# A graph attention kernel on one core: the slot table from one side of the comparison, and smaller first pieces of x and W_ah

## Chip, core and metric

One core of a Trainium2 chip. The metric is the device time of one execution in microseconds (us); runs of the same kernel are compared by their median.

## The reference

A graph network over N = 1250 nodes with D = 768 features and 41,250 edges (`src`, `dst`), the edges sorted by `dst`; the network adds a loop to every node.

```python
x1 = relu(x @ W_ah + b_ah)
for W, a_src, a_dst, b in three layers:           # 4 heads of 192 features
    h = (x1 @ W).reshape(N, 4, 192)
    e = leaky_relu((h * a_src).sum(-1)[src] + (h * a_dst).sum(-1)[dst], 0.2)
    alpha = softmax of e over the edges of each dst
    xs.append(relu(segment_sum(alpha * h[src], dst) + b))
y = relu(concatenate(xs) @ W_out + b_out)
out = layernorm(x + y)
```

## The kernel before

The attention is done densely: for each destination the kernel counts how often each source occurs (`cntT`, 1250 x 1250) and works with matrices after that. The start of the kernel makes these counts and, interleaved with them, x1.

*Counts.* The destinations are cut into NW = 105 windows of 12. Since the edges are sorted, the edges of a window are a run of the edge list. The **slot table** says where each window's run begins; 512 edges from there are loaded for each window (`load_slots`, L343, in 7 batches, the first of 4 windows). VectorE (DVE) turns them into key columns (`key_columns`, L853 to L861) and one-hot matrices (L865), two windows (one `unit`) at a time, three buffers deep. TensorE (PE) multiplies the one-hots into counts (L1131, L1148), ScalarE (ACT) moves the counts out (L580, L586).

*The slot table.* `dst` is loaded 330 edges to a partition, ten groups of 33. DVE takes the highest and the lowest destination of each group (L806, L807), compares them with every window's ends for two sides, the start of a run (side 0, `reaches[:, 0]`) and its end (side 1, `reaches[:, 1]`) (L808 to L811), and folds the ten groups to one (`reach`, L813 to L816). PE transposes both sides (L1181), DVE reduces over the partitions into `ab[:, 0:2]` (L820) and adds both for the run's length in `ab[:, 2]` (L822); PE lays both out as rows (L1184, L1185), and DVE makes the table from the first (L824). The second row, the lengths, is used only for the number of passes of a loop that takes edges beyond the 512 (L886 to L893).

*x1.* 108 steps (`x1_step`, L1172; six steps of 128 features to one output block, at two matmul instructions each). PE's order is written out by hand: two steps, the transposes of `reach`, the rows, steps up to the twelfth (`X1_HEAD`), and then a unit of counts, some steps, a unit, and so on, 53 units in all. ACT moves each finished block out (L604, L605) and asks for the W_ah piece after next.

*Queues.* ACT's DMA queue carries W_ah block 0 (L558, 384 KB), x for the first four tiles in three parts of 500 KB (L570; `G0_PARTS`) and W_ah block 1. SP's queue carries `dst` (L348) and two small biases, and, once the second x part is there, the vector a of layer 0 (L356, 768 KB) and the first 128 rows of W_all (L364, 384 KB). It then waits for the table and issues the edge loads.

*DVE's order* after the table: eight products of W_all with a (`reduce_v(0, 0)`, L839), then for each batch the key columns and one-hots; the loop counts come after batch 0. The other 136 products follow the last one-hot; PE's scores (L1209) wait for the last of them and for x1. The layers and the output follow.

Every step of DVE's table chain waits for the one before (`link`).

Of the kernel before, what the change touches and what calls it, by code (L numbers as in the profile page):

```python
# [14 lines left out]
PT = 125  # L15
NT = N // PT
KP = 128
KT = D // KP
LH = LAYERS * HEADS
WD = 12  # L20
NW = -(-N // WD)
# [22 lines left out]
G0_PARTS = 3  # L44
# [57 lines left out]
def gnn_program(nc, x, xT_rows, dst, edges, W_ah, b_ah, W_all, a_all, b_all, W_out, b_out, out):  # L102
# [10 lines left out]
    with ExitStack() as ctx:  # L113
# [3 lines left out]
        def sem(name):  # L117
            return ctx.enter_context(nc.semaphore(name))
# [180 lines left out]
        x0_in = [sem(f"x0_in{i}") for i in range(G0_PARTS)]  # L299
        x_in = [sem(f"x_in{g}") for g in range(len(GROUPS))]  # L300
        wah_in = [sem(f"wah_in{m}") for m in range(KT)]
# [45 lines left out]
        def _(sp):  # L347
            sp.dma_start(e_int, dst.rearrange("o (p e) -> p (o e)", p=PT)).then_inc(S["edges_in"], 16)  # L348
            sp.dma_start(b_ah_sb[:], b_ah).then_inc(S["small_in"], 16)
# [16 lines left out]
            sp.wait_ge(x0_in[G0_PARTS - 2], 16)  # L366
# [188 lines left out]
        def _(act):  # L555
# [10 lines left out]
            load_w_ah(0)  # L566
            for i in range(G0_PARTS):
                kk = slice(KT // G0_PARTS * i, KT // G0_PARTS * (i + 1))
                wide = GROUPS[0][1] * PT
                act.dma_start(xT[0][:, kk].rearrange("p k n -> p (k n)"),  # L570
                              xT_rows[:, kk.start * wide:kk.stop * wide]).then_inc(x0_in[i], 16)
# [216 lines left out]
        def _(dve):  # L788
            n = [0]

            def link(ins):
# [14 lines left out]
            link(nc.vector.tensor_reduce(highest, groups, axis=AX.X, op=ALU.max))  # L806
            link(nc.vector.tensor_reduce(lowest, groups, axis=AX.X, op=ALU.min))  # L807
            nc.vector.tensor_tensor(reaches[:, 0], over_w(highest), win_lo_g, ALU.is_ge)  # L808
            link(nc.vector.tensor_tensor(reaches[:, 1], win_hi_g, over_w(lowest), ALU.is_ge))
            nc.vector.tensor_tensor(reaches[:, 0], reaches[:, 0], over_w(to_end), ALU.mult)  # L810
            link(nc.vector.tensor_tensor(reaches[:, 1], reaches[:, 1], over_w(group_end), ALU.mult))  # L811
            rows = lambda v: v.rearrange("p s w g -> p (s w) g")
            link(nc.vector.tensor_tensor(rows(reach4), rows(reaches)[:, :, 0:4], rows(reaches)[:, :, 4:8], ALU.max))  # L813
            link(nc.vector.tensor_tensor(rows(reach2), rows(reach4)[:, :, 0:2], rows(reach4)[:, :, 2:4], ALU.max))
            link(nc.vector.tensor_tensor(rows(reach_g), rows(reach2), rows(reaches)[:, :, 8:GP], ALU.max))
            nc.vector.tensor_tensor(reach.rearrange("p s w -> p (s w)"), rows(reach_g)[:, :, 0], rows(reach_g)[:, :, 1],  # L816
                                    ALU.max).then_inc(S["reach_sb"], 1)

            dve.wait_ge(S["reachT_ps"], 1)
            link(nc.vector.tensor_reduce(ab[:, 0:2], bank(2)[0:NW, 0:256].rearrange("p (w c) -> p w c", w=2)[:, :, 0:PT],  # L820
                                         axis=AX.X, op=ALU.max))
            nc.vector.tensor_tensor(ab[:, 2:3], ab[:, 0:1], ab[:, 1:2], ALU.add).then_inc(S["ab_sb"], 1)  # L822
            dve.wait_ge(S["rows_ps"], 1)
            nc.vector.tensor_scalar(table[0:1, 0:NW], bank(3)[0:1, 0:NW], -float(GE), float(EDGES), ALU.mult, ALU.add  # L824
                                    ).then_inc(S["table_sb"], 1)

# [43 lines left out]
            for k in range(V_HEAD):  # L870
                reduce_v(0, k)
            dve.sem_inc(S["more_read"], 1)
            dve.wait_ge(S["consts_made"], 3)
            for i, (w0, mid, w1) in enumerate(BATCHES):
# [10 lines left out]
                if i == 0:  # L885
                    link(nc.vector.tensor_reduce(longest[0:1, 0:1], bank(3)[0:1, NW:2 * NW], axis=AX.X, op=ALU.max))  # L886
# [235 lines left out]
        def _(pe):  # L1122
# [36 lines left out]
            def x1_step(s):  # L1159

                i, k = s // KT, s % KT
                m, g = X1_ORDER[i]
                o, w = GROUPS[g][0] * PT, GROUPS[g][1] * PT
                if k == 0:
                    if i >= 3:
                        pe.wait_ge(S["turn_sb"], i - 2)
                    pe.wait_ge(wah_in[m], 16)
                    if g > 0:
                        pe.wait_ge(x_in[g], 16)
                if i == 0 and k % (KT // G0_PARTS) == 0:  # L1170
                    pe.wait_ge(x0_in[k // (KT // G0_PARTS)], 16)
# [262 lines left out]
```

## Time and profile before

| what | value |
|---|---|
| median of 3 runs | 964.36 us (963.82 to 965.69) |
| profiled execution, whole | 963.98 us |
| profiled execution, span from first to last instruction | 962.4 us |
| PE busy (matmuls) | 937.6 us, 97% of the span |
| DVE busy | 739.8 us, 77% |
| ACT busy | 366.8 us, 38% |

The span is what the trace covers; the rest of an execution's time lies around it. Shares of busy time are averages over stages with different limits, and a busy PE is one that has work in it, at whatever pace. In the rows below PE stands for matmuls and PEld for the weight loads that run beside them; SPq and ACTq are DMA issues on the queues of those engines.

### The profile page before, as it was taken

What the parts mean: (1) busy time and instruction counts of PE and PEld (TensorE: products, weight loads), DVE (VectorE), ACT (ScalarE), POOL (GpSimd) and SP (SyncE); (2) the same over time, 40 slices, a digit from 0 to 9 for tenths busy, and PEclk for the clock granted to TensorE, in tenths of its full rate; (3) what the DMA queues carried; (4) which work ended last, traced back from release to release, by engine and by line L of the source; (5) the groups of instructions that cost most, each with busy time, mean ns of one, the idle gap of its engine ahead of it and who ended that gap; (6) DMA issues with size and microseconds to landing.
All of it is one profiled execution on the core that took longest, in us unless ns stands there. A gap on an engine that the chain in (4) does not pass through costs nothing. (4 is left out here: it accounts for less than half of the span.)

```text
span 962.4 us, 14549 instructions
## 1 busy us (share of the span) xinstructions
PE 937.6 (97%) x5662; PEld 869.3 (90%) x5662; DVE 739.8 (77%) x1064; ACT 366.8 (38%) x534; POOL 45.8 (5%) x94
## 2 busy tenths in 40 slices
PE   6999999999999999999999999999999999999997
PEld 2677649999999999999999999999999879999996
DVE  6999986999999299989989988988877282243233
ACT  1566322122212245465555555555555450011000
POOL 4600000000000000010010010010010100000000
PEclk9999999999999999999999999999999999999999
DMA  6350722534442822153252362239331263223211
GB/s 181 55 183 19 259 85 91 165 115 143 140 153 89 229 82 82 64 126 79 84 120 62 93 130 58 78 87 375 101 103 60 87 169 129 81 85 113 75 33 32
DMA packets 57692, 108.16 MB, mean 112 GB/s; under 512 B 14012, under 2 KB 41245, under 8 KB 56486
## 3 DMA queue, kind: packets, MB, share of 16 engines
q1 hardware_dynamic: 39188, 66.22, 22.7%
q0 software_dynamic: 5360, 18.77, 8.0%
q10 hardware_dynamic: 13090, 22.44, 7.5%
q8 instruction: 34, 0.56, 0.2%
q14 instruction: 20, 0.16, 0.1%
HBM read 80.34 MB, written 27.08 MB: 112 GB/s over the span
## 5 line engine op out<-in xcount | busy, mean ns | idle before, releaser
L1311 PE MATMUL ps<-R_W 125*125 125x193 f32 x2400 | 397.8, 327 | 5.0 <-ACT R_XIN L722 3.9
L1311 PEld LDWEIGHTS ps<-R_W 125*125 125x125 f32 x2400 | 391.3, 188 | 8.7 <-ACT R_XIN L722 7.6
L707 ACT ACTIVATE R_W<-R_EXP,s 125x1250 f32<-125x1250 f32 x120 | 161.2, 1344 | 162.3 <-PE ps L1311 93.9
L998 DVE SCALAR_TENSOR_TENSOR R_W<-R_W,R_CNT 125x1250 f32<-125x1250 f32 x120 | 174.4, 1453 | 3.9 <-DVE R_EXP L987 2.0
L957 DVE CUSTOM_DVE_ANT_0 R_ROWS<-R_MASK,R_ROWS 125x1250 bf16<-125x1250 bf16 x100 | 138.6, 1453 | 3.2 <-ACTq L660 3.2
L1228 PE MATMUL ps<-Wl_hi,x_hi 128*125 128x384 f32 x360 | 122.1, 339 | 0.0
L1228 PE MATMUL ps<-Wl_hi,x_lo 128*125 128x384 f32 x360 | 121.7, 338 | 0.0
L1228 PE MATMUL ps<-Wl_lo,x_hi 128*125 128x384 f32 x360 | 121.6, 338 | 0.0
L1370 PE MATMUL ps<-Wo_hi,xs_hi 128*125 128x384 f32 (+2 forms) x324 | 109.5, 338 | 0.3 <-PE ps L1360 0.3
L1370 PE MATMUL ps<-Wo_lo,xs_hi 128*125 128x384 f32 (+2 forms) x324 | 109.4, 338 | 0.0
L1370 PE MATMUL ps<-Wo_hi,xs_lo 128*125 128x384 f32 (+2 forms) x324 | 109.2, 337 | 0.0
L987 DVE SCALAR_TENSOR_TENSOR R_EXP<-R_EXP,s 125x1250 f32<-125x1250 f32 x60 | 90.7, 1514 | 21.1 <-DMA R_EXP<-u_dram 12.2
L987 DVE SCALAR_TENSOR_TENSOR R_EXP<-R_X,s 125x1250 f32<-125x1250 f32 x60 | 90.6, 1510 | 18.4 <-ACT R_W L707 18.0
L1102 DVE TENSOR_TENSOR R_EXP<-ps,R_EXP 125x768 f32<-125x768 f32 (+2 forms) x11 | 9.7, 884 | 99.0 <-PE ps L1370 99.0
L680 ACT COPY R_HOUT<-ps 125x384 f32<-125x384 f32 x60 | 28.9, 481 | 140.3 <-PE ps L1228 138.7
L1172 PE MATMUL ps<-R_W 128*128 128x500 f32 (+1 forms) x180 | 73.8, 540 | 7.6 <-DMA R_W<-in_xT 7.6
L1228 PEld LDWEIGHTS ps<-Wl_hi,x_hi 128*125 128x125 f32 x360 | 66.8, 185 | 0.5 <-issue 0.4
L1228 PEld LDWEIGHTS ps<-Wl_lo,x_hi 128*125 128x125 f32 x360 | 66.7, 185 | 0.0
L1228 PEld LDWEIGHTS ps<-Wl_hi,x_lo 128*125 128x125 f32 x360 | 66.7, 185 | 0.0
L785 ACT ACTIVATE rstd<-mv,epsc 125x1 f32<-125x1 f32 x10 | 3.0, 295 | 158.6 <-DVE mv L1113 158.6
L865 DVE TENSOR_TENSOR R_EXP<-R_EXP 128x2000 f16<-128x2000 f16 (+1 forms) x53 | 59.7, 1185 | 2.7 <-PE ps L1148 2.4
L1370 PEld LDWEIGHTS ps<-Wo_hi,xs_hi 128*125 128x125 f32 x324 | 60.0, 185 | 1.8 <-issue 0.9
(146 smaller groups left out, 854.0 us busy)
## 6 DMA issues: line engine op xcount, KB each, us to landing
xs_dram<-R_XIN POOLq DMA_DIRECT2D x18, 625.0 KB, 9.3
h_dram<-R_HOUT ACTq DMA_DIRECT2D x30, 336.0 KB
R_W<-h_dram SPq DMA_DIRECT2D x12, 840.0 KB
R_ROWS<-as_dram SPq DMA_DIRECT2D x12, 625.0 KB, 4.4
R_EXP<-u_dram SPq DMA_DIRECT2D x6, 1250.0 KB, 6.4
R_X<-u_dram SPq DMA_DIRECT2D x6, 1250.0 KB, 5.8
R_ROWS<-in_W_all SPq DMA_DIRECT2D x18, 384.0 KB, 3.5
Wo_sb<-in_W_out POOLq DMA_DIRECT2D x1, 6912.0 KB, 27.3
```

Source lines behind the costliest of these rows:

```text
L680: nc.scalar.copy(h_out[:, slot, t % 2 * HALF:(t % 2 + 1) * HALF], bank((2 * c + t) % 4)[0:PT, 0:HALF]).then_inc(S["h_sb"], 1)
L707: nc.scalar.activation(prob[r % PSLOTS], expo[:, r % XSLOTS], ACT.Exp, bias=s02[:, r % NT, ds(2 * p + r // NT, 1)]).then_inc(S["exp_done"], 1)
L785: nc.scalar.activation(rstd[:, t % 2, 0:1], mv[:, t % 2, 1:2], ACT.Sqrt, bias=epsc[:, 0:1]).then_inc(S["std_done"], 1)
L865: return nc.vector.tensor_tensor(slot.rearrange("p (b q c) -> p b q c", b=blocks, c=EPR), cols.unsqueeze(1).broadcast_to((KP, blocks, PT * ...
L957: nc.vector.tensor_tensor_reduce(out=masked[:, i % 2], in0=mask[:, b], in1=asB[0:PT, hh % 2], scale=1.0, scalar=NOBODY, op0=ALU.add, op1=A ...
L987: nc.vector.scalar_tensor_tensor(out=expo[:, r % XSLOTS], in0=uB[q][0:PT, 0], scalar=s08[:, r % NT, ds(2 * p + q, 1)], in1=uB[q][0:PT, 1], ...
L998: nc.vector.scalar_tensor_tensor(out=prob[r % PSLOTS], in0=prob[r % PSLOTS], scalar=HUGE, in1=cntT[:, r % NT, 0:N], op0=ALU.min, op1=ALU.m ...
L1102: nc.vector.tensor_tensor(yt_part, y_part, bo_part, ALU.add).then_inc(S["y_sum"], 1)
L1172: ins = mm(bank(5 + i % 3)[:, 0:w], W_ah_sb[m][:, k], xT[g][:, k], start=(k == 0), stop=(k == KT - 1))
L1228: ins = mm(place, xx[:, k, t * PT:(t + 1) * PT], ww[n][:, k], start=(k == 0 and i == 0), stop=(k == blocks[-1] and i == 2), skip_group_che ...
L1311: ins = mm(ps[0:PT, o:o + HW], prob[r % PSLOTS][:, t * PT:(t + 1) * PT], hB[:, q, j], start=(j == 0 and t % 2 == 0), stop=(j == NT - 1), s ...
L1370: ins = mm(place, xx[i][:, k], ww[:, k, half], start=(k == 0 and n == 0), stop=(k == OK - 1 and n == 2))
```

## The change

The table is made from side 0 alone, and side 1, with the lengths, is worked out behind it. W_ah block 0 is loaded in two pieces: its first 128 columns of the 768 in front of x on ACT's queue, the rest on SP's queue behind `dst`. The first x group comes in four parts, of 1, 1, 2 and 2 of its six blocks, where there were three parts of 2. PE does four x1 steps ahead of the first transpose where it did two, the second transpose after nine, and the row of lengths after twelve. DVE folds each side by itself, compares side 1 between the first reduction and the table, and reduces and adds the lengths after `reduce_v(0, 0)`.

```diff
-G0_PARTS = 3
+X0_CUTS = (0, 1, 2, 4, 6)
+X0_PARTS = list(zip(X0_CUTS, X0_CUTS[1:]))
+BEFORE_TABLE = 4
+BEFORE_LENGTHS = 9
...
             sp.dma_start(e_int, dst.rearrange("o (p e) -> p (o e)", p=PT)).then_inc(S["edges_in"], 16)
+            sp.dma_start(W_ah_sb[0][:, 1:KT].rearrange("p k f -> p (k f)"), W_ah[0][:, KP:KT * KP]).then_inc(wah_in[0], 16)
...
-            sp.wait_ge(x0_in[G0_PARTS - 2], 16)
+            sp.wait_ge(x0_in[len(X0_PARTS) - 2], 16)
...
-            load_w_ah(0)
-            for i in range(G0_PARTS):
-                kk = slice(KT // G0_PARTS * i, KT // G0_PARTS * (i + 1))
+            act.dma_start(W_ah_sb[0][:, 0], W_ah[0][:, 0:KP]).then_inc(wah_first, 16)
+            for i, (k0, k1) in enumerate(X0_PARTS):
                 wide = GROUPS[0][1] * PT
-                act.dma_start(xT[0][:, kk].rearrange("p k n -> p (k n)"),
-                              xT_rows[:, kk.start * wide:kk.stop * wide]).then_inc(x0_in[i], 16)
+                act.dma_start(xT[0][:, k0:k1].rearrange("p k n -> p (k n)"),
+                              xT_rows[:, k0 * wide:k1 * wide]).then_inc(x0_in[i], 16)
...
+            def fold(side):
+
+                link(nc.vector.tensor_tensor(reach4[:, side], reaches[:, side, :, 0:4], reaches[:, side, :, 4:8], ALU.max))
+                link(nc.vector.tensor_tensor(reach2[:, side], reach4[:, side, :, 0:2], reach4[:, side, :, 2:4], ALU.max))
+                link(nc.vector.tensor_tensor(reach_g[:, side], reach2[:, side], reaches[:, side, :, 8:GP], ALU.max))
+                nc.vector.tensor_tensor(reach[:, side], reach_g[:, side, :, 0], reach_g[:, side, :, 1], ALU.max
+                                        ).then_inc(S["reach_sb"], 1)
+
+            link(nc.vector.tensor_tensor(reaches[:, 0], over_w(highest), win_lo_g, ALU.is_ge))
+            link(nc.vector.tensor_tensor(reaches[:, 0], reaches[:, 0], over_w(to_end), ALU.mult))
+            fold(0)
             link(nc.vector.tensor_reduce(lowest, groups, axis=AX.X, op=ALU.min))
...
+            dve.wait_ge(S["reachT_ps"], 1)
+            nc.vector.tensor_reduce(ab[:, 0:1], bank(2)[0:NW, 0:PT], axis=AX.X, op=ALU.max).then_inc(S["ab_sb"], 1)
             link(nc.vector.tensor_tensor(reaches[:, 1], win_hi_g, over_w(lowest), ALU.is_ge))
...
             dve.wait_ge(S["rows_ps"], 1)
             nc.vector.tensor_scalar(table[0:1, 0:NW], bank(3)[0:1, 0:NW], -float(GE), float(EDGES), ALU.mult, ALU.add
                                     ).then_inc(S["table_sb"], 1)
+            link(nc.vector.tensor_tensor(reaches[:, 1], reaches[:, 1], over_w(group_end), ALU.mult))
+            fold(1)
...
             for k in range(V_HEAD):
                 reduce_v(0, k)
+            dve.wait_ge(S["reachT_ps"], 2)
+            dve.wait_ge(S["ab_sb"], 1)
+            link(nc.vector.tensor_reduce(ab[:, 1:2], bank(2)[0:NW, 128:128 + PT], axis=AX.X, op=ALU.max))
+            nc.vector.tensor_tensor(ab[:, 2:3], ab[:, 0:1], ab[:, 1:2], ALU.add).then_inc(S["ab_sb"], 1)
...
                 if i == 0:
+                    dve.wait_ge(S["rows_ps"], 2)
...
-                    pe.wait_ge(wah_in[m], 16)
+                    pe.wait_ge(wah_first if i == 0 else wah_in[m], 16)
...
+                if i == 0 and k == 1:
+                    pe.wait_ge(wah_in[0], 16)
+                if i == 0 and k in X0_CUTS:
+                    pe.wait_ge(x0_in[X0_CUTS.index(k)], 16)
...
-            for s in range(KT // G0_PARTS):
+            for s in range(BEFORE_TABLE):
                 x1_step(s)
-            pe.wait_ge(S["reach_sb"], 1)
-            for w in range(2):
-                ins = nc.tensor.transpose(bank(2)[0:NW, w * 128:w * 128 + PT], reach[:, w], ident[0:PT, 0:PT])
-            ins.then_inc(S["reachT_ps"], 1)
-            pe.wait_ge(S["ab_sb"], 1)
-            mm(bank(3)[0:1, 0:NW], ab[:, 0:1], ident[0:NW, 0:NW], start=True, stop=True)
-            mm(bank(3)[0:1, NW:2 * NW], ab[:, 2:3], ident[0:NW, 0:NW], start=True, stop=True).then_inc(S["rows_ps"], 1)
-
-            for s in range(KT // G0_PARTS, X1_HEAD):
+            reach_turn(0)
+            table_row(0)
+            for s in range(BEFORE_TABLE, BEFORE_LENGTHS):
                 x1_step(s)
+            reach_turn(1)
+            for s in range(BEFORE_LENGTHS, X1_HEAD):
+                x1_step(s)
+            table_row(2)
```

`reach_turn(side)` waits for `reach` of that side and transposes it; `table_row(column)` waits for that column of `ab` and lays it out as a row.

## Rows read from the trace of the kernel before

**Rows 1.** The chain that ended last, page, share of the span by engine.

```profile
PE 24%; ACT 0%; DVE 0%; issue 0%; ACTq 0%
```

**Rows 2.** Timeline, loads and first steps: start, duration, instruction, idle and releaser.

```profile
0.97 0.38 SPq L348 DMA_DIRECT2D R_CNT<-in_dst  x1
...
1.40 1.43 ACTq L570 DMA_DIRECT2D R_W<-in_xT  x3
...
7.58 3.67 PE L1172 MATMUL ps<-R_W 128*128 128x500 f32 x4 [7.58 <-DMA R_W<-in_xT]
...
8.54 0.34 PEld L1172 LDWEIGHTS ps<-R_W 128*128 128x128 f32 x1 [0.50 <-issue]
8.71 0.33 SPq L356 DMA_DIRECT2D R_ROWS<-in_a_all  x1
...
9.38 0.34 PEld L1172 LDWEIGHTS ps<-R_W 128*128 128x128 f32 x1 [0.50 <-issue]
```

**Rows 3.** Timeline, DVE from dst to reach.

```profile
5.66 0.33 DVE L804 CAST R_CNT<-R_CNT 125x330 f32<-125x330 int32 x1 [1.19 <-DMA R_CNT<-in_dst]
6.02 0.50 DVE L806 TENSOR_REDUCE R_CNT<-R_CNT 125x10 f16<-125x330 f32 x1
...
7.08 0.71 DVE L808 TENSOR_TENSOR R_CNT<-R_CNT 125x1050 f16<-125x1050 f16 x1
...
9.80 0.62 DVE L813 TENSOR_TENSOR R_CNT<-R_CNT 125x840 f16<-125x840 f16 x1
10.46 0.38 DVE L814 TENSOR_TENSOR R_CNT<-R_CNT 125x420 f16<-125x420 f16 x1
10.87 0.54 DVE L815 TENSOR_TENSOR R_CNT<-R_CNT 125x420 f16<-125x420 f16 x1
11.44 0.38 DVE L816 TENSOR_TENSOR R_CNT<-R_CNT 125x210 f32<-125x210 f16 x1
```

**Rows 4.** Timeline, the exchange between PE and DVE for the table.

```profile
11.87 0.46 PE L1181 MATMUL ps<-ident,R_CNT 125*105 125x125 f32 x2 [0.62 <-DVE R_CNT L816]
12.37 0.42 DVE L820 TENSOR_REDUCE ab<-ps 105x2 f32<-105x250 f32 x1 [0.55 <-PE ps L1181]
12.83 0.16 DVE L822 TENSOR_TENSOR ab<-ab 105x1 f32<-105x1 f32 x1
...
13.49 8.65 PE L1172 MATMUL ps<-R_W 128*128 128x500 f32 x20
13.60 0.26 DVE L824 TENSOR_SCALAR table<-ps 1x105 int32<-1x105 f32 x1 [0.61 <-PE ps L1185]
```

**Rows 5.** Timeline, DVE from the table to the loop counts.

```profile
15.26 0.36 DVE L839 CUSTOM_DVE_ANT_0 R_EXP<-R_ROWS 128x192 bf16<-128x192 f32 x1 [1.41 <-DMA R_ROWS<-in_W_all]
...
17.51 0.07 DVE L839 DVE_READ_ACCUMULATOR2_ANT u_place<- 128x1 f32 x1
...
18.04 0.18 DVE L853 CAST R_EXP<-R_EXP 128x32 f32<-128x32 int32 x1 [0.46 <-DMA R_EXP<-in_edges]
...
19.21 2.31 DVE L865 TENSOR_TENSOR R_EXP<-R_EXP 128x2000 f16<-128x2000 f16 x2
...
21.44 0.25 DVE L886 TENSOR_REDUCE longest<-ps 1x1 int32<-1x105 f32 x1
```

**Rows 6.** Timeline, PE at unit 0, units 2 and 6, and the scores.

```profile
21.98 0.39 PE L1131 MATMUL ps<-R_EXP 128*125 128x120 f16 x4
...
25.19 0.45 PE L1131 MATMUL ps<-R_EXP 128*125 128x120 f16 x4 [0.97 <-DVE R_EXP L865]
...
31.02 0.42 PE L1131 MATMUL ps<-R_EXP 128*125 128x120 f16 x4 [0.50 <-DVE R_EXP L865]
...
129.96 12.77 PE L1209 MATMUL ps<-R_X,u_place 128*24 128x500 f32 x36 [0.49 <-issue]
```

**Rows 7.** Waits of DVE, 31.1 to 132 us; one window, busy by engine.

```profile
DVE R_EXP L865 <- PE ps L1148: 2.4, 6, 0.9
...
31.10:150.00 118.90, 118.37 (x847) 79.41 (x848) 108.90 (x356) 58.64 (x110) 11.13 (x38) 1.00 0.41 127
```

More of the change, by code:

```diff
@@ L298, in gnn_program @@
         S = {n: sem(n) for n in names}
-        x0_in = [sem(f"x0_in{i}") for i in range(G0_PARTS)]
+        x0_in = [sem(f"x0_in{i}") for i in range(len(X0_PARTS))]
         x_in = [sem(f"x_in{g}") for g in range(len(GROUPS))]
+        wah_first = sem("wah_first")
         wah_in = [sem(f"wah_in{m}") for m in range(KT)]
@@ L807, in _ @@
+            link(nc.vector.tensor_tensor(reaches[:, 0], over_w(highest), win_lo_g, ALU.is_ge))
+            link(nc.vector.tensor_tensor(reaches[:, 0], reaches[:, 0], over_w(to_end), ALU.mult))
+            fold(0)
             link(nc.vector.tensor_reduce(lowest, groups, axis=AX.X, op=ALU.min))
-            nc.vector.tensor_tensor(reaches[:, 0], over_w(highest), win_lo_g, ALU.is_ge)
+            dve.wait_ge(S["reachT_ps"], 1)
+            nc.vector.tensor_reduce(ab[:, 0:1], bank(2)[0:NW, 0:PT], axis=AX.X, op=ALU.max).then_inc(S["ab_sb"], 1)
@@ L809, in _ @@
             link(nc.vector.tensor_tensor(reaches[:, 1], win_hi_g, over_w(lowest), ALU.is_ge))
[L810 to L821, printed above, removed]
@@ L822, in _ @@
-            nc.vector.tensor_tensor(ab[:, 2:3], ab[:, 0:1], ab[:, 1:2], ALU.add).then_inc(S["ab_sb"], 1)
             dve.wait_ge(S["rows_ps"], 1)
@@ L1166, in x1_step @@
                         pe.wait_ge(S["turn_sb"], i - 2)
-                    pe.wait_ge(wah_in[m], 16)
+                    pe.wait_ge(wah_first if i == 0 else wah_in[m], 16)
                     if g > 0:
                         pe.wait_ge(x_in[g], 16)
-                if i == 0 and k % (KT // G0_PARTS) == 0:
-                    pe.wait_ge(x0_in[k // (KT // G0_PARTS)], 16)
+                if i == 0 and k == 1:
+                    pe.wait_ge(wah_in[0], 16)
+                if i == 0 and k in X0_CUTS:
+                    pe.wait_ge(x0_in[X0_CUTS.index(k)], 16)
                 ins = mm(bank(5 + i % 3)[:, 0:w], W_ah_sb[m][:, k], xT[g][:, k],
@@ L1175, in x1_step, with reach_turn, table_row @@
                     ins.then_inc(S["turn_ps"], 1)
-            for s in range(KT // G0_PARTS):
-                x1_step(s)
-            pe.wait_ge(S["reach_sb"], 1)
-            for w in range(2):
-                ins = nc.tensor.transpose(bank(2)[0:NW, w * 128:w * 128 + PT], reach[:, w], ident[0:PT, 0:PT])
-            ins.then_inc(S["reachT_ps"], 1)
-            pe.wait_ge(S["ab_sb"], 1)
-            mm(bank(3)[0:1, 0:NW], ab[:, 0:1], ident[0:NW, 0:NW], start=True, stop=True)
-            mm(bank(3)[0:1, NW:2 * NW], ab[:, 2:3], ident[0:NW, 0:NW], start=True, stop=True).then_inc(S["rows_ps"], 1)
-            for s in range(KT // G0_PARTS, X1_HEAD):
+            def reach_turn(side):
+                pe.wait_ge(S["reach_sb"], side + 1)
+                nc.tensor.transpose(bank(2)[0:NW, side * 128:side * 128 + PT], reach[:, side], ident[0:PT, 0:PT]
+                                    ).then_inc(S["reachT_ps"], 1)
+            def table_row(column):
+                pe.wait_ge(S["ab_sb"], 1 if column == 0 else 2)
+                o = 0 if column == 0 else NW
+                mm(bank(3)[0:1, o:o + NW], ab[:, column:column + 1], ident[0:NW, 0:NW], start=True, stop=True
+                   ).then_inc(S["rows_ps"], 1)
+            for s in range(BEFORE_TABLE):
+                x1_step(s)
+            reach_turn(0)
+            table_row(0)
+            for s in range(BEFORE_TABLE, BEFORE_LENGTHS):
                 x1_step(s)
+            reach_turn(1)
+            for s in range(BEFORE_LENGTHS, X1_HEAD):
+                x1_step(s)
+            table_row(2)
             for un in range(NU):
```

## The prediction

> **What bounds the kernel now.** I read the chain of waits first. It follows back only the last quarter of the span, all of it in the output product [rows 1], so it says nothing of the start, where the whole edit lies. So I took the timeline from 0 to 45 us, engine by engine, and then asked where the start meets the rest: the waits of PE and DVE behind it, and the busy time of a long window.
>
> The start is three threads. PE cannot begin before the first x piece lands, at 7.58 us; it does two steps, stops for `reach` at 11.87, stops again for `ab`, and runs ten steps from 13.49 [rows 2, 4]. DVE gets `dst` at 5.66, finishes both sides of `reach` at 11.82 (11.44 + 0.38), and writes the table from 13.60 to 13.86 [rows 3, 4]. Behind the table stand the edge loads, and DVE takes up the first edges at 18.04. Meanwhile it does the eight products on W_all, from 15.26, when W_all has landed, to 17.58 [rows 5]. The reader should see that DVE is free only 0.46 us before the edges are there.
>
> From 18.04 DVE runs without a break into the one-hots (19.21), the loop counts (21.44) and the next batch. PE reaches unit 0 at 21.98, although its one-hots were ready near 20.4 (19.21 and half of 2.31). But then it waits 0.97 us for DVE before 25.19, and 0.50 before 31.02 [rows 6]. So up to 31 us DVE sets the pace. From there PE is busy 118.37 of 118.90 us, while DVE waits for PE six times, 2.4 us in all [rows 7]. Both meet again at 129.96, where PE stands 0.49 us [rows 6]: the scores need DVE's last product. What the edit does to the end is therefore how far it moves DVE's first key columns, now at 18.04, and with them one-hots and PE at 31 us. The rest hangs on that like a rigid bar.
>
> **The change part by part.**
>
> *Loads.* Step 0 needed 384 + 500 KB of the ACT queue, beside 173 KB on SP's: 1057 KB in all by 7.58 us. `x0_in[1]`, 500 KB on, lets SP issue at 8.71 [rows 2]: 442 KB per us. `dst` (161 KB, with at least as much of the other queue beside it) was usable at 5.66 [rows 3], which makes 383 KB per us up to 7.58. Step 0 now needs 64 + 250 KB, with as much moved for SP (`dst`, then the 320 KB rest of W_ah): 628 KB, hence 5.66 + 306/383 = 6.5 us. Bounds: 5.7 (as early as `dst`) and 7.6 (no gain). Step 1 needs x part 1 and the W_ah rest, 1057 KB again, so 7.6; step 0 runs until 8.2 and hides that. Steps 2 and 3 need what let SP issue at 8.71 and start later. The bytes ahead of the a and W_all loads are the same and SP's wait names the same x rows, so I keep W_all at 15.26. Bounds: 0.5 us earlier (two queues full from the start) and 0.3 later (smaller pieces).
>
> *PE ahead of the table.* A slow step costs 2 x 0.84 = 1.67 us (weight loads at 8.54 and 9.38 [rows 2]); the steps from 13.49 are twice as fast, 20 instructions in 8.65 us, less their tail 0.42 each, 0.84 a step [rows 4]. These are the paces of the two levels, 1.2 and 2.4 GHz. PE was slow from 7.58 at least until its fourth matmul, which began near 10.2, some 3.67 us of work in all. I let it be slow for 3.8 us again: from 6.5, two steps at 1.67 (9.84), step 2 half and half (1.25, 11.09), step 3 0.84: 11.93. `reach_turn(0)` then comes at 11.93, where the transposes now start at 11.87: the head start is spent on the two added steps.
>
> *DVE ahead of the table.* `reach` of side 0 is ready long before: highest (ends 6.52), comparison and product 2 x 0.71, then the four folds at half size, about 9.4 us with gaps of 0.03 [rows 3]. That 2.4 us gain goes into waiting for PE. Fold prices: 840 elements took 0.62 and 420 took 0.38, so 0.57 ns an element on 0.14 fixed; the halves cost 0.38, 0.26, 0.34 (from 0.54) and 0.26 (from 0.38), 1.24 instead of 0.96 for half the work.
>
> The Trainium skill, "VectorE: DVE Perf Modes", section "The TRN2 errata", speaks against such a split: operations out of SBUF pay a fixed extra time per instruction, so small tiles should be avoided. The rows agree (the 0.14 above); if the time went by elements alone, the sum below would be 0.28 smaller.
>
> *The exchange.* Now from 11.87: reduction at 12.37, sum 0.16, table at 13.60. After: one transpose, reduction at 11.93 + 0.31 = 12.24 for about 0.28 (half of 0.42, plus the fixed part), to 12.52. Then the comparison of side 1, 0.71, sits between reduction and table on DVE: to 13.22. The row comes back from PE 0.43 after the reduction (the 0.61 of now, 12.99 to 13.60, less two matmuls), at 12.95, hidden. Table 13.25 to 13.51: **0.35 us earlier** than 13.86. Edges land as long after it as now (4.18): 17.69.
>
> *DVE behind the table.* Moved here: product 0.70, four folds 1.24, five gaps 0.15: 2.09, ends 15.60. W_all is there at 15.26, so the eight products (2.32) run 15.60 to 17.92. Then the second reduction 0.28, the sum 0.16 and their gaps 0.06: 18.42. The edges have landed. The key columns start near 18.45, **0.4 us later than 18.04**. So the gap DVE stood idle in (13.86 to 15.26, 17.58 to 18.04, 1.86 us) is filled with 2.59 us of moved work, and only 0.35 is won by the early table.
>
> *New waits.* `reach_turn(1)` stands on PE behind nine steps, about 17.2 (12.95 and five steps); side 1 is ready at 15.6, and the transpose is there at 17.5 when DVE asks for it at 17.92, 0.4 to spare. `table_row(2)` waits for `ab` at 18.4, and PE gets there after three more steps and the transpose, near 19.8; its row, at 20.1, is wanted only by DVE's loop counts, at 21.44 + 0.4. Queued behind it stand PE's units, whose first one-hots are ready at 20.8. So all three cost nothing, and from the named slack on they cost what is over. ACT's third W_ah piece goes out earlier, with block 0, and may slow the 4 KB edge loads; they have 0.7 us to spare.
>
> Sum: +0.4 us. The profiled execution took 963.98 us (span 962.4, 1.6 around it), so 964.4; the median of the runs lies 0.4 above that one: **964.8 us**. Ends of the terms: PE starting at 5.7 leaves W_all as the bound, 15.26 + 2.32 + 0.5 = 18.1, +0.05, and with W_all 0.5 earlier -0.4. PE starting at 7.6 puts the table 1.1 later: +1.5. Other terms are worth 0.1 to 0.2.
>
> **Rivals.**
>
> *A, PE's head start counts.* PE loses two gaps and starts 1.1 us sooner, so unit 0 can start at 20.8 for 21.98, 1.2 us earlier; with quicker DMA at most 1.6. If PE's order set the pace, 963.2 (962.8). For it: PE is nearly always busy from 13.49 on. Against: the 0.97 and 0.50 it waits for DVE [rows 6].
>
> *B, the bar is not DVE.* If the folds hid better than I think, or W_all came early, the table's 0.35 would pass through with the edges: 964.0, and if W_all is simply the bound, 964.4, the change doing nothing.
>
> *C, PE is later at the table.* All four steps slow: 6.5 + 6.68 = 13.18 instead of 11.93, +1.25 and so +1.65: 966.0. Four PE steps now stand before the first transpose where two stood.
>
> The Trainium skill, "TensorE: Matmul & The Clock Gate", Part 1, says that the throttled clock is the default, that activity releases it, and that the point of release varies from run to run. No run here shows that yet; it would make C a matter of luck, with 964.8 in lucky runs.
>
> *D, over the bound of "same".* The low clock lasts until about 18 us. Then PE is 4 us later at `table_row(2)` than 19.8, past the 21.8 at which DVE wants the row: +2.0 and up to +6 if it lasts through all twelve steps (6.5 + 20.0 + 1.5 = 28.0). It decides from 1.9 us on. For it: two queues might make PE stop between its first steps. Against: step 1's data lands before step 0 ends.
>
> **How the numbers follow.** Forecast (-0.1 to +0.9 us around the median) 0.60; A 0.11; B 0.13; C 0.10; D 0.06. What a measurement of this kernel can tell is about 0.2%, 1.9 us. Faster than that would need A with everything early and a little more: 0.06. Slower by more is D and the tail of C with the spread of the runs: 0.08. The rest, 0.86, is the same. The range goes from A (963.2) to C with the spread of a median (966.2).
>
> **What would show it.** Right: first matmul 6.2 to 6.8; DVE idle from about 10 to 12.2; table end near 13.5; products on W_all starting at the end of the folds, 15.3 to 15.8; key columns 18.1 to 18.8; PE waiting over 1.5 us before unit 2, and everything from 31 us shifted by the same few tenths. Wrong: the table before 12.8, or W_all well before 15, or PE at 31 us moved otherwise than DVE's key columns; or a shift that is undone or doubled where the two engines meet near 130 us.

## The result: 1.8 us slower, and the profile after

The changed kernel takes 966.72 us, the kernel before 964.94 (medians of 20 runs each); the ratio is 1.0017, 95% interval 1.0010 to 1.0024. I had forecast 964.8 with a range up to 966.2. The direction of my sum was right, its size was not: 0.4 forecast, 1.8 measured, which is 0.17% and beyond what I allowed. One of the 20 runs of the changed kernel took 2766.8 us at full clock, which no trace explains; without it the median is 966.68. The profiled execution took 966.63 us with a span of 965.0, 2.6 longer than that of before.

A *stand* is below a time in which an engine waits and does nothing. Times at which a load landed and times at which the clock changed are read from the records of the traces, where no line is shown for them.

The timeline of the changed kernel, first the loads and PE and DVE up to the table:

```profile
5.22 0.33 DVE L808 CAST R_CNT<-R_CNT 125x330 f32<-125x330 int32 x1 [0.75 <-DMA R_CNT<-in_dst]
...
6.62 5.46 PE L1185 MATMUL ps<-R_W 128*128 128x500 f32 x8 [6.62 <-DMA R_W<-in_xT]
...
7.60 0.40 DVE L814 TENSOR_TENSOR R_CNT<-R_CNT 125x420 f16<-125x420 f16 x1
8.03 0.27 DVE L815 TENSOR_TENSOR R_CNT<-R_CNT 125x210 f16<-125x210 f16 x1
8.33 0.35 DVE L816 TENSOR_TENSOR R_CNT<-R_CNT 125x210 f16<-125x210 f16 x1
8.59 0.33 SPq L361 DMA_DIRECT2D R_ROWS<-in_a_all  x1
8.72 0.27 DVE L817 TENSOR_TENSOR R_CNT<-R_CNT 125x105 f32<-125x105 f16 x1
...
11.92 0.27 PE L1193 MATMUL ps<-ident,R_CNT 125*105 125x125 f32 x1
12.29 0.29 DVE L825 TENSOR_REDUCE ab<-ps 105x1 f32<-105x125 f32 x1 [2.90 <-PE ps L1193]
12.50 0.70 DVE L826 TENSOR_TENSOR R_CNT<-R_CNT 125x1050 f16<-125x1050 f16 x1
...
13.23 0.26 DVE L828 TENSOR_SCALAR table<-ps 1x105 int32<-1x105 f32 x1
```

These answer to [rows 2 to 4], and they agree with the forecast nearly to the digit: PE starts at 6.62 (forecast 6.5), the transpose comes at 11.92 (11.93), the table is done at 13.49 (13.51), 0.37 earlier than before. Side 0 is ready at 8.99 and its transpose starts at 11.92; DVE, which has one more reduction to do, stands 2.90 us for it. W_all, which I had kept at 15.26, landed at 13.9 in this trace, but DVE asked for it only at 15.44, behind the moved work.

The same timeline behind the table, against [rows 5, 6]:

```profile
15.03 0.33 ACTq L563 DMA_DIRECT2D R_W<-in_W_ah  x1
15.25 0.27 DVE L817 TENSOR_TENSOR R_CNT<-R_CNT 125x105 f32<-125x105 f16 x1
15.44 0.35 DVE L845 CUSTOM_DVE_ANT_0 R_EXP<-R_ROWS 128x192 bf16<-128x192 f32 x1
...
17.98 0.16 DVE L881 TENSOR_TENSOR ab<-ab 105x1 f32<-105x1 f32 x1
19.14 0.18 DVE L859 CAST R_EXP<-R_EXP 128x32 f32<-128x32 int32 x1 [1.00 <-DMA R_EXP<-in_edges]
...
20.39 2.31 DVE L871 TENSOR_TENSOR R_EXP<-R_EXP 128x2000 f16<-128x2000 f16 x2
...
21.64 0.45 PE L1142 MATMUL ps<-R_EXP 128*125 128x120 f16 x4 [1.37 <-DVE R_EXP L871]
...
22.75 0.45 PE L1142 MATMUL ps<-R_EXP 128*125 128x120 f16 x4 [0.34 <-DVE R_EXP L871]
...
24.29 0.20 DVE L859 CAST R_EXP<-R_EXP 128x64 f32<-128x64 int32 x1 [0.67 <-DVE table L904]
...
26.87 0.45 PE L1142 MATMUL ps<-R_EXP 128*125 128x120 f16 x4 [2.42 <-DVE R_EXP L871]
...
33.67 0.39 PE L1142 MATMUL ps<-R_EXP 128*125 128x120 f16 x4
...
132.62 12.77 PE L1233 MATMUL ps<-R_X,u_place 128*24 128x500 f32 x36 [0.51 <-issue]
```

DVE is through with the moved work at 18.14 (forecast 18.42), but now it stands 1.00 us for the edges. ACT's load of W_ah block 2 (384 KB) goes out at 15.03. In the kernel before it was this line of the timeline:

```profile
17.29 0.33 ACTq L558 DMA_DIRECT2D R_W<-in_W_ah  x1
```

The windows of the changed kernel show this load running just when SP's last edge load of the first batch, issued at 15.80, is under way: 346 GB/s in the row below. That edge load landed 3.25 us after its issue (15.80 to 19.05); in the kernel before it took 1.78 (16.17 to 17.95).

```profile
core 0: us, PE busy (x) PEld busy (x) DVE busy (x) ACT busy (x) POOL busy (x), PEclk, DMA share, GB/s
...
16.50:17.50 1.00, 1.00 (x5) 0.52 (x4) 1.00 (x9) 0.98 (x2) 0.68 (x2) 1.00 0.90 346
```

The windows further on show a third thing. The column to read is PEclk, the granted share of TensorE's clock:

```profile
24.50:27.40 2.90, 0.53 (x9) 0.53 (x9) 2.74 (x7) 0.09 (x1) 2.34 (x5) 1.00 0.24 14
27.50:30.90 3.40, 3.40 (x17) 2.25 (x15) 3.30 (x8) 0.34 (x1) 2.81 (x6) 0.50 0.23 15
31.00:34.00 3.00, 3.00 (x31) 2.09 (x30) 2.93 (x5) 1.62 (x4) 2.14 (x4) 1.00 0.26 18
```

PE stood 1.37 us ahead of unit 0 and 2.42 us ahead of unit 2; from 27.5 to 30.9 it is granted 0.50, its 1.2 GHz level, in full work. So the 2.65 us of this execution come together as follows. The key columns start 1.10 later (18.04 to 19.14). Unit 2 starts 1.68 later (25.19 to 26.87); 0.44 of the additional 0.58 is a longer stand of DVE ahead of the second batch, batch 1 (0.67 for 0.23), and 0.14 is small change. Unit 6 starts 2.65 later (31.02 to 33.67), the 0.97 more being slow matmuls. From there all is rigid, as forecast: the scores start at 132.62 (+2.66), and in every trace below except that of `e8_steps` the span ends 832.3 to 832.5 us after them.

### The profile page after: what moved, and what is told of

It reads as the page before. It is cut to its first block and busy times, and to the rows that moved or that the text cites. A ratio compares the mean times of both kernels' runs of the same rounds, so it can differ in the third digit from the quotient of the medians.

```text
span 965.0 us, 14560 instructions
## 1 busy us (share of the span) xinstructions
PE 939.4 (97%) x5662; PEld 870.7 (90%) x5662; DVE 740.8 (77%) x1069; ACT 366.7 (38%) x534; POOL 45.8 (5%) x94
## 5 line engine op out<-in xcount | busy, mean ns | idle before, releaser
L998 DVE SCALAR_TENSOR_TENSOR R_EXP<-R_EXP,s 125x1250 f32<-125x1250 f32 x60 | 90.9, 1516 | 21.0 <-DMA R_EXP<-u_dram 12.5
```

The costliest lines, as they stand in the source:

```text
L998: nc.vector.scalar_tensor_tensor(out=expo[:, r % XSLOTS], in0=uB[q][0:PT, 0], scalar=s08[:, r % NT, ds(2 * p + q, 1)], in1=uB[q][0:PT, 1], ...
```

## The experiments

Medians are of 10 to 12 runs of each kernel, with runs of the kernel before on the same chip between them (21 to 33, medians 964.75 to 964.97); `e11_before_again` and `e12_after_again` are one run each. The ratio comes with its interval from the runs of a series and is not exactly the quotient of the medians. What is said of a trace holds for one execution.

**The W_ah load held back.** `e1_hold`, below called the held kernel, is the changed kernel in which ACT waits for the first batch of edges before it asks for W_ah block 2:

```diff
+                if i == 0:
+                    act.wait_ge(win_in[0], 16 * (BATCHES[0][1] - BATCHES[0][0]))
                 if i + 2 < KT:
                     load_w_ah(i + 2)
```

> The changed kernel, but ACT holds its load of W_ah block 2 (384 KB) until the first batch's edges have landed; nothing else is different. Theory 1 (collision, then clock): the block's load, issued at 15.03 us instead of 17.29, delays the 4 KB edge loads by about 1.4 us. Then the first edges land by 17.8 us, DVE's first key columns start at 18.4 (my old sum) instead of 19.14, PE stands about 1.7 us before unit 2 instead of 2.4, and the time is 0.3 to 0.7 us over the kernel before if the clock does not fall, 1.3 to 1.6 over it if it still does. Theory 2 (the edges are late for another reason, SP's issues or W_all itself): edges still land near 19.1 and the time stays about 1.8 us over the kernel before.

```profile
18.34 0.18 DVE L861 CAST R_EXP<-R_EXP 128x32 f32<-128x32 int32 x1
...
20.74 0.45 PE L1144 MATMUL ps<-R_EXP 128*125 128x120 f16 x4 [0.29 <-DVE R_EXP L873]
```

The key columns start at 18.34, the last edge load landing 1.81 us after its issue: the collision is shown, and with it gone my old sum holds (+0.30 for +0.4). But the median is 966.46, ratio 1.0015 (1.0006 to 1.0024), so of the 0.80 us that the key columns win only 0.26 is seen in the medians, and the intervals of the two ratios overlap. The spans of the eleven runs go from 963.3 to 966.6: four runs at a mean clock of 0.998 have 963.3 to 963.9, the seven at 0.997 or less 964.3 to 966.6. The profiled run is one of the four, and its clock did not fall near unit 2. That the other seven had such a fall is likely but not shown. The mean is a weak witness, since it also counts the last microseconds of the span, in which PE has no more work (0.50 from 959.8 on in this trace), and in the kernel before the runs with a mean of 0.997 or less are not the long ones (all but one of 25 have spans of 962.4 to 963.3).

**The same load early in the kernel before.** `e2_early`:

```diff
-                if i + 2 < KT:
+                if 0 < i < KT - 2:
                     load_w_ah(i + 2)
-                elif i + 2 - KT < len(GROUPS) - 1:
+                elif 0 <= i + 2 - KT < len(GROUPS) - 1:
                     load_x(i + 3 - KT)
...
             act.wait_ge(S["small_in"], 32)
+            act.wait_ge(S["table_sb"], 1)
+            load_w_ah(2)
             x1_out(0)
-            act.wait_ge(S["table_sb"], 1)
```

> The kernel before, but ACT issues its load of W_ah block 2 right when the table is ready (13.9 us) instead of behind the first x1 block (17.29). Nothing of the change is in it. Theory 1: the first edges land 1 to 1.5 us later than 18.04, key columns near 19.2, PE stands 2.0 to 2.4 us before unit 2, and the kernel is 1.0 us slower than before, or 2 and more where PE's clock falls behind that stand. Theory 2 (the moved DVE work does it): this kernel is as fast as before, within 0.3 us.

The median is 965.33 us, ratio 1.0000 (0.9991 to 1.0009). In time this is a miss for theory 1. The load, issued at 14.69, landed at 17.75, 0.84 us after the last edge load was issued (the edge loads were issued from 15.33 to 16.91); in the changed kernel it landed 2.40 after that. The last edge load took 2.17 us. The trace of `e9_before_late` below has its table and its edge loads at the same times to 0.02 us and no such load beside them: there the last edge load took 1.92, and the key columns start at 18.93 for 19.17 here. So a W_ah load that is early by this much costs 0.24 us; what the collision costs depends on how far the load lands behind the issue of the last edges.

**The two halves of the change.** `e3_loads` is the kernel before with the pieces of W_ah and x alone, `e4_table` the changed kernel without them:

```diff
+            sp.dma_start(W_ah_sb[0][:, 1:KT].rearrange("p k f -> p (k f)"), W_ah[0][:, KP:KT * KP]).then_inc(wah_in[0], 16)
...
-            load_w_ah(0)
-            for i in range(G0_PARTS):
...
+            act.dma_start(W_ah_sb[0][:, 0], W_ah[0][:, 0:KP]).then_inc(wah_first, 16)
+            for i, (k0, k1) in enumerate(X0_PARTS):
```

The second has these lines the other way round, against the changed kernel.

> The kernel before with only the load part of the change: W_ah block 0 in two pieces on two queues, x in four parts; table and PE order as before (two steps, both transposes, both rows). PE starts at 6.6, dst at 5.2, so reach is ready at 11.4, 0.4 earlier, the table near 13.45, W_ah block 2 is issued near 16.9. Theory 1: edges land 0.3 to 0.5 earlier or, brushing the W_ah load, at 18.0; time -0.4 to +0.1 against before. If the loads themselves are the harm (two queues, smaller pieces), W_all lands later than 15.3 and the time is 0.5 or more over before.

> The changed kernel with the old loads: table from side 0, four steps ahead of it, side 1 behind, but W_ah block 0 and x as before. PE starts at 7.58, so the four steps end near 13.0 and the table near 14.5. The W_ah block 2 load goes out near 16.1, after most edge loads. DVE's chain behind the table (4.9 us) puts the key columns at 19.3 to 19.6. Theory 1 and my old sum agree on +1.3 to +1.6 us from that; a fall of PE's clock would add 1 us. If the split of the table were harmless and only the loads hurt, the time would be that of before.

Loads only: 964.78, ratio 0.9995 (0.9986 to 1.0004), no harm and no gain. Its trace has a sign that I had named for harm, a late W_all (timeline, DVE's first product):

```profile
16.47 0.36 DVE L841 CUSTOM_DVE_ANT_0 R_EXP<-R_ROWS 128x192 bf16<-128x192 f32 x1 [2.55 <-DMA R_ROWS<-in_W_all]
```

Its table and its key columns were late too (13.92 and 18.71, the clock rising only at 19.0), but its span (963.4) does not follow them. W_all landed between 13.9 and 16.3 us in the traces with the new loads and between 15.1 and 16.0 in those with the old ones, so where it lands differs from run to run.

Table only: 967.24, ratio 1.0025 (1.0016 to 1.0034), +2.5. The loss is in the table part; that the loads give some 0.5 of it back is not clear of the intervals. Its table was at 14.41 and its key columns at 20.07, later than the 19.6 I allowed: the W_ah load (issued at 15.95) met the last edge load (issued 16.72, landed 19.98). Its clock fell too, from 28.6 to 32.0, behind stands of PE of 1.38 us ahead of unit 0 and 2.41 ahead of unit 2.

**The stand of DVE ahead of batch 1.** It is there in all six traces that have the new DVE order, the loop counts behind batch 0 and no padding. All edges of the batch have landed (20.50 and 21.41 in the changed kernel, DVE starts at 24.29), and it always stands behind the 63rd DVE record of the trace, waits counted. `e7_pad`, below called the padded kernel, is the held kernel with nine waits that are long satisfied:

```diff
+            for _ in range(9):
+                dve.wait_ge(S["consts_made"], 1)
             dve.wait_ge(S["edges_in"], 16)
```

> The held kernel with nine waits more on DVE ahead of dst, all long satisfied, 0.02 us each in idle time. In the three kernels with the new table order DVE stands 0.5 us ahead of batch 1's key columns, at the same place of its program (64 instructions in) and with all edges of the batch landed. If the stand hangs on the count of instructions, the padding moves it under the long one-hots of batch 0, and unit 2 starts 0.4 to 0.5 us sooner than in the held kernel (25.5 for 25.94); time 0.3 to 0.5 lower. If it hangs on data or on another engine, nothing moves.

Timeline of the held kernel, DVE and PE, and of the padded one:

```profile
23.39 0.28 DVE L861 CAST R_EXP<-R_EXP 128x64 f32<-128x64 int32 x1 [0.67 <-DVE table L906]
...
25.94 0.45 PE L1144 MATMUL ps<-R_EXP 128*125 128x120 f16 x4 [2.39 <-DVE R_EXP L873]
```

```profile
22.96 0.20 DVE L863 CAST R_EXP<-R_EXP 128x64 f32<-128x64 int32 x1 [0.23 <-DVE table L908]
...
25.54 0.45 PE L1146 MATMUL ps<-R_EXP 128*125 128x120 f16 x4 [1.97 <-DVE R_EXP L875]
```

Nine idle waits make DVE 0.43 us quicker, with the key columns of batch 0 at the same place (18.36 for 18.34). So the stand hangs on the place in DVE's list of instructions and not on data. A further sign is in the DMA records: an 8 KB packet of the queue named instruction starts at 20.67 in the padded kernel's trace, while DVE is in its one-hots, and the held kernel's has none from 19 us until 23.99. Whose instructions it carried the trace doesn't say, so that DVE waits for its own instructions here is likely and not shown. The median is 965.51 us, ratio 1.0006 (0.9995 to 1.0016), 0.95 below the held kernel; that is more than the 0.4 in the trace, and the intervals of the two overlap. Only 4 of its 11 runs have a mean clock of 0.997 or less, where 7 of 11 had.

**The clock.** `e5_filler`, on the changed kernel, puts idle matmuls into PE's stand:

```diff
+                if un == 2:
+                    for _ in range(30):
+                        mm(bank(4)[:, 0:128], ident16[:], ident16[:], start=True, stop=True)
                 unit(un)
```

> The changed kernel with 30 small matmuls more on PE (128 x 128, f16, into a bank that nobody reads) right ahead of unit 2, where PE stood 2.42 us; about 2 us of PE work in the place of idle time. It computes nothing that is used. If the fall of PE's clock to 1.2 GHz at 27.5 us follows from that stand, the clock stays at 2.4 GHz, unit 6 starts near 32.7 instead of 33.67 and the time is about 1.0 us below the changed kernel (965.7 against 966.7), the key columns unchanged near 19.1. If the clock falls for another reason, or its fall costs nothing, the time is that of the changed kernel.

In its trace the clock stays up, and unit 2 to unit 6 take 5.90 us (27.58 to 33.48) instead of 6.80, nearly as before the change (5.83). But unit 6 starts only 0.19 earlier than in the changed kernel (33.67), since the key columns were not where I had expected them: the clock rose at 12.7 in this run, not at 10.4, and they start at 19.99 for 19.14. And the median is 968.10, ratio 1.0031 (1.0018 to 1.0044): the expected gain isn't there, and part of its runs are 2 us slower than any cause above explains. The fall's price is shown by the trace, a cure in this form is not. Nor does one trace without a fall show that the filling prevented it, since PE's stand ahead of unit 0 was shorter too (1.03).

`e11_before_again` and `e12_after_again` are the kernel before and the changed one, unedited.

> The kernel before, unchanged, for a second trace of it. If the point at which PE's clock rises is a matter of the run and not of the kernel, it will not be at 11.4 us again; 16.9 was seen in a kernel with the same start. Then PE reaches unit 0 up to 2 us later and the time hardly changes, since DVE sets the pace there. If the rise follows from what PE did, it is at 11.4 again.

> The changed kernel, unchanged, for a second trace of it. The first had the clock rise at 10.4 us and fall to 1.2 GHz from 27.5 to 30.9. Expected: W_ah block 2 issued right behind the first x1 block, first edges 3.2 us or more after their last issue again, the 0.5 us stand ahead of batch 1; whether the clock rises late (12.7, the table 1.1 us later, as in two relatives) or falls near unit 2 (1.0 us) is open, and each run should have at least one of the two if these two make the spread of its runs.

Timeline of the kernel before, second trace:

```profile
7.68 3.67 PE L1172 MATMUL ps<-R_W 128*128 128x500 f32 x4 [7.68 <-DMA R_W<-in_xT]
...
14.45 10.99 PE L1172 MATMUL ps<-R_W 128*128 128x500 f32 x20
14.56 0.26 DVE L824 TENSOR_SCALAR table<-ps 1x105 int32<-1x105 f32 x1 [0.95 <-PE ps L1185]
```

The ten steps took 10.99 us where they took 8.65 [rows 4]: PE worked at 1.2 GHz until 19.2 us (the clock record of the trace; 11.4 in the first). The same program is 1.7 us longer in its span (964.1). I had expected the time hardly to change, since DVE would set the pace. It did not in this run: the table came 0.96 later, and PE reached unit 0 at 25.28, 3.3 later, and had no stand from there to unit 6 (32.47, 1.45 later). `dst` landed 0.34 later too, so not all of the 1.7 is the clock's. The first trace of before was one of its quickest runs. The Trainium skill, "TensorE: Matmul & The Clock Gate", Part 1, says that this point differs from run to run; the two traces agree: 11.4 and 19.2, which is a far wider spread than the half microsecond to either side that the page gives.

The changed kernel, second trace, timeline and windows:

```profile
24.89 0.20 DVE L859 CAST R_EXP<-R_EXP 128x64 f32<-128x64 int32 x1 [0.66 <-DVE table L904]
27.36 0.45 PE L1142 MATMUL ps<-R_EXP 128*125 128x120 f16 x4 [2.30 <-DVE R_EXP L871]
```

```profile
25.00:28.40 3.40, 1.10 (x12) 0.90 (x12) 3.23 (x9) 0.20 (x1) 2.80 (x6) 1.00 0.22 13
28.50:31.90 3.40, 3.40 (x14) 1.93 (x13) 3.23 (x9) 1.03 (x2) 2.68 (x5) 0.50 0.26 16
```

Again there is a late edge load (issued 16.56, landed 19.74), the stand of 0.66, PE standing 1.22 ahead of unit 0 and 2.30 ahead of unit 2, the clock at its low level for 3.4 us, and unit 2 to unit 6 in 6.81. With the clock's rise at 11.4 like the first trace of before, its span is 966.1 against 962.4.

**More PE work into the stand.** Two x1 steps are moved ahead of unit 2, in the padded kernel (`e8_steps`) and in the kernel before (`e10_before_steps`):

```diff
-    return X1_HEAD + 3 * (u + 1) // 4
+    return X1_HEAD + 3 * (u + 1) // 4 + (2 if u >= 1 else 0)
```

> The held and padded kernel with two x1 steps (1.7 us of PE work) moved from later to just ahead of unit 2, where PE stands about 2 us for DVE. The work is the same, only its order. If PE's stand there makes its clock fall in part of the runs, the slow end of the runs (965 and more in 4 of 11 spans of the padded kernel) goes away: median 0.6 to 1.2 us below the padded kernel's 965.5. If the falls have nothing to do with the stand, the spread stays as it was and only up to 0.5 us is won from PE's shorter list behind 31 us.

> The kernel before with the same two steps moved ahead of unit 2. There PE stood only 0.97 us, so unit 2 comes 0.7 us later or, where the clock rose late, 1.7 us later, and then PE has 1.7 us less to do. If PE's order were the bound from 31 us on, the gain and the loss cancel: within 0.5 us of the kernel before.

`e8_steps`: 964.92, ratio 1.0000 (0.9992 to 1.0009), 0.6 below the padded kernel and at the lower end of what I expected. Nine of its 11 spans lie between 962.6 and 964.0. Two have 966.0 and 968.0, where four of the padded kernel's had 964.7 to 965.8; so few runs don't show that the long ones come from unit 2. The longest is the profiled one; its timeline (DVE's waits among its last products, then PE) and windows:

```profile
112.60 0.36 DVE L849 CUSTOM_DVE_ANT_0 R_EXP<-R_ROWS,R_HOUT 128x192 bf16<-128x192 f32 x1 [1.04 <-DMA R_ROWS<-in_W_all]
...
121.90 0.36 DVE L849 CUSTOM_DVE_ANT_0 R_EXP<-R_ROWS 128x192 bf16<-128x192 f32 x1 [1.75 <-DMA R_ROWS<-in_W_all]
...
133.26 1.00 PE L1237 MATMUL ps<-R_X,u_place 128*24 128x500 f32 x1 [4.32 <-issue]
```

```profile
131.20:138.10 6.90, 4.84 (x7) 1.13 (x8) 4.83 (x17) 0.00 (x0) 0.00 (x0) 0.51 0.41 148
138.10:145.00 6.90, 6.90 (x21) 2.05 (x20) 4.68 (x4) 0.00 (x0) 0.00 (x0) 1.00 0.00 0
```

PE is ahead of DVE at the scores, stands 4.32 us for the last product, and its clock falls there, from 131.25 on. But the two steps are the smaller part of this stand. PE's x1 work ends 1.0 us earlier than in the padded kernel (128.94 for 129.90), while DVE's last product starts 2.7 later (132.79 for 130.10), because DVE waited 2.8 us for loads of W_all and 0.7 more where the padded kernel's trace has one such wait of 1.0. Why those loads were late in this run is not shown.

`e10_before_steps`: 967.07, ratio 1.0026 (1.0016 to 1.0035), a miss. Unit 2 came at 27.67 and unit 6 at 32.78, and nothing came back later: from unit 6 to the scores 99.1 us, as before (98.9), PE standing 1.89 us for DVE's last product at their start. The profiled run is the quickest of its ten (span 964.2), with a late rise of the clock (16.7) like the second trace of before (964.1); what makes the others longer than that is not shown.

**The loop counts out of DVE's way.** `e9_before_late` on the kernel before, `e6_late_longest` on the held one, `e16_late_again` the latter once more (the wait for `rows_ps` is not in the kernel before):

```diff
-                if i == 0:
+                if i == 1:
                     dve.wait_ge(S["rows_ps"], 2)
                     link(nc.vector.tensor_reduce(longest[0:1, 0:1], bank(3)[0:1, NW:2 * NW], axis=AX.X, op=ALU.max))
+                if i == 3:
                     link(nc.vector.tensor_scalar(longest[0:1, 1:2], longest[0:1, 0:1], GE, MORE - 1 - SLOT - EDGES,
```

> The kernel before with the loop counts moved as in the run before the last, and nothing of the change. If DVE's chain sets the end, PE no longer stands 0.97 us before unit 2 and at most 0.4 before unit 6, and the time is 0.8 to 1.2 us below the kernel before. If PE's order sets the end, no change.

> The changed kernel with the held W_ah block 2, and DVE's loop counts moved: the reduction of the lengths behind batch 1 instead of batch 0, the five small operations behind batch 3, where DVE waits for PE anyway. It takes 1.2 us out of DVE's chain ahead of unit 2, and the 0.5 us stand ahead of batch 1's key columns if that hangs on the place in DVE's program. Theory (DVE's chain up to 31 us sets the end): unit 2 at 24.3, unit 6 near 30.2, time 0.5 to 0.9 us below the kernel before, 1.5 to 2.5 below the held kernel. If PE's order sets the end, the time stays that of the held kernel.

> The kernel with the held W_ah block 2, four steps and late loop counts once more, beside the last on the same chip: 0.3 to 0.5 us below the kernel before as in its first series, no run with a fall of the clock ahead of 60 us.

On the kernel before: 964.93, ratio 0.9997 (0.9987 to 1.0007), no gain. Unit 6 was at 31.23 although the clock rose only at 16.9, but from there to the scores it took 99.66 us instead of 98.94, PE standing 0.8 for DVE at the end. DVE has the same work in another order, so it reaches its last product no earlier. On the held kernel: 964.53 in both series, ratios 0.9991 (0.9983 to 1.0000) and 0.9993 (0.9985 to 1.0002), spans 961.8 to 963.7 in all 22 runs, none of them long; up to unit 6 PE stands 0.9 us at most in either trace, and the clock does not fall there. That is 2.2 us below the changed kernel and 0.2 to 0.35 below the kernel before, less than the 0.5 to 0.9 that I expected of the first series, and the intervals hardly tell it from nothing.

**Two steps ahead of the table instead of four.** `e14_two` on the changed kernel, `e15_two_late` on the kernel of the last run:

```diff
-BEFORE_TABLE = 4
+BEFORE_TABLE = 2
```

> The changed kernel with two x1 steps ahead of the first transpose instead of four, nothing else. Theory (the four steps spend the head start and tie the table to the run's clock): the transpose comes at 6.6 + 3.4 = 10.0, the table near 11.6 whatever the clock does, the first edges land near 15.8, before ACT's W_ah block 2 load can meet them; DVE's key columns then follow W_all: 15.5 + 2.8 = 18.3. The 0.5 us stand ahead of batch 1 stays. Time 0.7 to 1.6 us below the changed kernel, that is level with the kernel before or up to 0.8 over it. If the four steps do no harm, the time is that of the changed kernel, 1.8 over.

> The kernel with the held W_ah block 2 and the late loop counts, now with two steps ahead of the first transpose. Table near 11.6 in every run, key columns 18.3, no stand ahead of batch 1, DVE 1.2 us shorter: one-hots of unit 2 at 23.0, unit 6 near 29.6 to 30.2 (31.02 before). Time 0.8 to 1.6 us below the kernel before, with runs closer together than its relatives. If the end hangs on something else than DVE's chain to unit 6, it stays at the 964.5 of the kernel with four steps.

The timeline of `e14_two`, and one window:

```profile
11.50 0.26 DVE L828 TENSOR_SCALAR table<-ps 1x105 int32<-1x105 f32 x1
...
16.23 0.36 DVE L845 CUSTOM_DVE_ANT_0 R_EXP<-R_ROWS 128x192 bf16<-128x192 f32 x1 [2.44 <-DMA R_ROWS<-in_W_all]
...
21.42 0.45 PE L1142 MATMUL ps<-R_EXP 128*125 128x120 f16 x4 [1.21 <-DVE R_EXP L871]
```

```profile
23.60:30.40 6.80, 5.04 (x24) 2.76 (x23) 6.09 (x13) 0.77 (x2) 5.26 (x11) 0.50 0.25 15
```

The table is 2.1 us earlier than before and nothing comes of it. In this run W_all binds (DVE's products start at 16.23, in the first trace of before at 15.26), the key columns start at 18.97, and PE's clock is at 0.50 from 23.6 to 30.4. It had fallen before PE stood ahead of unit 2 (from 24.8 to 26.5), behind the stand of 1.21 ahead of unit 0 and one of 0.35. The median is 967.05 us, ratio 1.0021 (1.0012 to 1.0029), where I had expected 0.7 to 1.6 below the changed kernel: taking two of the four steps away brings nothing. `e15_two_late`: 965.65, ratio 0.9998 (0.9989 to 1.0008), in two groups, five spans at 961.5 to 962.4 and seven at 964.1 to 965.8. The waits of DVE in the profiled one, of the second group:

```profile
DVE ab L882 <- PE ps L1196: 3.1, 1, 3.1
```

Its clock rose at 16.4, the nine steps ahead of side 1's transpose ran slow, and DVE stood 3.1 us for it, ahead of its key columns (20.71). This is the wait that I had given 0.4 us to spare.

## Why the prediction was wrong

*Right.* That what is late at unit 6 is late at the end, all behind it shifting like a bar; the start of PE, the table's 0.35 us, the fold prices (0.40, 0.27, 0.35, 0.27 for 0.38, 0.26, 0.34, 0.26), the price of the moved work. With the collision away the key columns came 0.30 late for 0.4. That the new loads by themselves leave the time where it was (`e3_loads`) was right as well.

*Right in part.* That DVE's chain sets the pace up to unit 6 holds for the first trace of before. In the changed kernel it holds up to unit 2, and then PE at its low clock sets it; in the second trace of before PE sets it from unit 0 on. W_all was not where I had kept it: it landed at 13.9 (15.1 before), which was one of my signs of being wrong ("W_all well before 15"), but DVE had no use for it before 15.44, so it cost and gave nothing.

*Wrong, the step on new waits.* "ACT's third W_ah piece goes out earlier ... and may slow the 4 KB edge loads; they have 0.7 us to spare." It cost them 1.5 (3.25 for 1.78), so the key columns were 1.10 late and not 0.4. I had seen the collision and put it at nothing without looking for a price. That PE ends block 0 early was in my own sums (two steps behind 12.95, 14.6), and my own 383 KB per us gives the load 1.0 us of transfer, an estimate that is already more than the 0.7 to spare.

*Wrong, "everything from 31 us shifted by the same few tenths".* I forecast over 1.5 us of stand ahead of unit 2 and counted PE's stands as nothing, since PE was not the bound there. With 1.2 to 1.4 us of stand ahead of unit 0 and 2.3 to 2.4 ahead of unit 2 the clock fell in both traces of the changed kernel and in that of `e4_table`. It cost 0.97 to 0.98 us each time (6.80, 6.81 and 6.81 from unit 2 to unit 6 for 5.83), and by then PE was the bound. The stand ahead of unit 2 is not enough by itself: the held kernel's trace has 2.39 us of it, only 0.29 ahead of unit 0, and no fall; `e14_two` has 1.21 ahead of unit 0 and its fall before unit 2. The stand ahead of unit 0 comes from the late edges, so the collision, which I had put at nothing, probably had a hand in the fall as well. What exactly the clock answers to is not shown. My rival D looked for a low clock only at the start.

*Not foreseen.* The longer stand, by 0.44 us, at a fixed place of DVE's program.

*Of luck.* Two traces of the same kernel, with the clock's rise early and late, differ by 1.7 us (before, 11.4 and 19.2) and 1.1 (changed, 10.4 and 11.4). Not all of it is the clock's, as the loads differ too. My sum stood on a trace of before with an early rise.

The trace of the changed kernel is accounted for: 1.10 + 0.44 + 0.97 + 0.14 = 2.65. The medians differ by only 1.8, probably because runs of before hold late rises too. How much of the 1.8 each cause has isn't settled: the held kernel, the padded one and the one with late counts are 0.3, 1.2 and 2.2 below the changed kernel, but each step also changes the length of PE's stands. Why part of the runs of `e5_filler` are so slow stays open, and what DVE does in its stand is not shown.

## What to carry to other kernels

When work is taken out of one engine's way at the start, follow what the faster engine releases: here PE finished its first block earlier, and the load that ACT issues behind it met the one transfer that all waited for. Idle time of an engine off the bound was not free here, where that engine was TensorE and became the bound soon after. And before a prediction rests on one trace of a start, have a second: the same program gave 962.4 and 964.1 us.

## What the runs showed of the hardware

- The clock rose in the same program at 11.4 and at 19.2 us, and in its relatives between 9.9 and 19.2.
- It fell to 1.2 GHz in three traces behind stands of PE of 1.2 to 1.4, 0.35 and 2.3 to 2.4 us with little work between them, and stayed there 3.4 us. It fell behind stands of 1.2 and 0.35 (`e14_two`) and in one of 4.3 (`e8_steps`), and stayed there 6.8 us. Stands of 0.29, 0.35 and 2.39 (`e1_hold`) left it up.
- Four-KB edge loads took 1.8 to 2.0 us from issue to landing with no large load on the other queue, and 3.0 to 3.3 where a 384 KB load landed 2.3 to 2.5 us behind the issue of the last of them; where it landed 0.8 behind it they took 2.2. In `e14_two`, where they were issued from 12.5 to 14.1 while W_all was still on its way on their own queue (landed at 16.1), the last took 3.3.
- DVE stood 0.66 to 0.67 us, for 0.23 elsewhere, behind the 63rd record of its trace, and nine satisfied waits ahead of it took the difference away.
